# Attention inside a four-block kernel: the row maximum is subtracted by TensorE in PSUM instead of by VectorE

## The reference

```python
qkv = win @ w_qkv + b_qkv                       # win: (256 windows, 49, 32)
attn = jnp.einsum('whnd,whmd->whnm', q, k) * scale
attn = jax.nn.softmax(attn, axis=-1)            # over the 49 keys
out = jnp.einsum('whnm,whmd->whnd', attn, v)
out = out @ w_proj + b_proj
```

## Time and profile before

| | us |
|---|---|
| median of 3 runs (470.24 to 478.76) | 473.28 |
| the profiled execution, its own time | 475.85 |
| its span in the profile | 474.1 |
| mean granted TensorE clock | 0.901 |
| busy: PE, DVE, ACT, POOL | 351.1, 365.1, 299.8, 233.9 |

### The profile page before, as it was taken

The page is one execution under the profiler, slowest core; times in us unless marked ns, Lnnn a source line. Parts: engine busy times, 40 slices in busy tenths (PEclk is TensorE's granted clock), DMA queues, the critical chain, the costliest instruction groups (busy, mean ns, idle before and its releaser), DMA issues. The chain is left out here.

```text
span 474.1 us, 10021 instructions
## 1 busy us (share of the span) xinstructions
PE 351.1 (74%) x3480; PEld 230.4 (49%) x3480; DVE 365.1 (77%) x679; ACT 299.8 (63%) x583; POOL 233.9 (49%) x217
## 2 busy tenths in 40 slices
PE   5149888896789785985877647666795829888885
PEld 4037676675665332142233213222483519877774
DVE  3799999999797388799787999997576685544443
ACT  4327788887785899578758946347985253333432
POOL 4526868775673324966972999567081130000000
PEclk9997999998899999599897885768999668999999
DMA  6110000000223231022000000000030000111111
GB/s 147 5 18 3 3 1 0 0 1 0 59 60 70 51 87 29 1 60 58 1 0 1 0 1 0 0 0 1 3 68 3 1 0 11 20 19 22 22 19 24
DMA packets 24044, 10.29 MB, mean 22 GB/s; under 512 B 20576, under 2 KB 22368, under 8 KB 24016
## 3 DMA queue, kind: packets, MB, share of 16 engines
q1 hardware_dynamic: 23888, 9.93, 10.3%
q0 software_dynamic: 128, 0.01, 0.2%
HBM read 2.00 MB, written 1.61 MB: 8 GB/s over the span
## 5 line engine op out<-in xcount | busy, mean ns | idle before, releaser
L480 POOL TENSOR_TENSOR Pr<-Pr,rc 128x392 f32<-128x392 f32 x64 | 54.4, 883 | 32.2 <-DVE rc L1826 32.2
L511 POOL TENSOR_TENSOR YA<-YA,hC 128x784 f32<-128x784 f32 x27 | 51.7, 1914 | 32.4 <-DVE hC L1910 31.5
L1349 PE MATMUL pair<-BCf,sel 96*128 96x392 bf16 x128 | 38.4, 394 | 35.0 <-DVE Hs L1894 30.8
L1894 DVE TENSOR_TENSOR_SCAN Hs<-dA,pair 128x784 f32<-128x784 f32 x32 | 57.1, 1785 | 1.0
L1193 PE MATMUL pair<-ident,Pr 128*128 128x128 f32 x256 | 41.1, 293 | 13.2 <-ACT PT L715 9.0
L1349 PEld LDWEIGHTS pair<-BCf,sel 96*128 96x128 bf16 x128 | 10.2, 105 | 74.0 <-issue 71.6
L1193 PEld LDWEIGHTS pair<-ident,Pr 128*128 128x128 f32 x256 | 29.2, 146 | 25.1 <-ACT PT L715 15.8
L1887 DVE TENSOR_TENSOR pair<-DU,pair 128x784 f32<-128x784 f32 x32 | 31.1, 973 | 10.6 <-PE pair L1349 10.3
L715 ACT ACTIVATE PT<-pair 128x392 f32<-128x392 f32 x64 | 31.4, 497 | 5.9 <-PE pair L1193 5.6
L724 ACT ACTIVATE Pr<-Ts 128x392 f32<-128x392 f32 x64 | 32.5, 536 | 3.4 <-DVE Ts L1810 3.4
L1804 DVE TENSOR_REDUCE mx<-pair 128x8 f32<-128x392 f32 x64 | 32.6, 550 | 1.6 <-PE pair L1150 1.4
(11 more groups left out here) (262 smaller groups left out, 928.8 us busy)
## 6 DMA issues: line engine op xcount, KB each, us to landing
SX<-XP SPq DMA_DIRECT2D x48, 112.2 KB
XT<-in_x SPq DMA_DIRECT2D x4, 392.0 KB, 5.0
out<-Os SPq DMA_DIRECT2D x28, 56.0 KB, 1.8
AD<-Aa SPq DMA_DIRECT2D x4, 196.0 KB
NB<-in_L_conv_x_proj_w SPq DMA_DIRECT2D x4, 3.0 KB
DW<-in_L_conv_dw SPq DMA_DIRECT2D x4, 1.1 KB
vec<-in_L_conv_b_qkv POOLq DMA_DIRECT2D x3, 0.5 KB, 5.8
W<-in_L_conv_w_qkv SPq DMA_DIRECT2D x1, 48.0 KB
```

The costliest lines, as they stand in the source:

```text
L480: eng.tensor_tensor(pg, pg, bcast(rc[:, g, :], 2, WT), ALU.mult).then_inc(pn_r, 1)
L511: eng.tensor_tensor(y, y, hC[:, n % NHC, :], ALU.add).then_inc(g_ya, 1)
L1349: ins = eng.matmul(SPREAD[s][:, columns(h)], sel[:, n, :], upper(BCf[:, c % 2, s, columns(h)]), start=True, stop=True)
L1894: eng.tensor_tensor_scan(Hs[:, n % 2, :], dA[:, n % NA, :], SPREAD[0], 0.0, ALU.mult, ALU.add).then_inc(v_s, 1)
```

## The change

The subtraction on DVE, its output tile `Ts` and its semaphore `sub_r` go. In their place, for each part of two groups: PE turns the maxima (`mx`, now 32 columns a part, 16 used) with an identity in float32, twice, into two 32-row blocks of bank 7 (`turn_max`); DVE copies the 64 rows to the bfloat16 tile `MT`, and then overwrites rows 32 to 63 by what the rounding left (`pieces`); PE multiplies `MT` by a fixed bfloat16 matrix `msel` of 0 and -1 and adds the product onto the scores in banks 2 * part and 2 * part + 1 (`shift`). ACT takes the exponent from PSUM. The banks of the scores are given back by the exponent. ACT's order becomes t0, t1, t2, e0, t3, e1, e2, e3; PE's new steps stand between the transposes; DVE's order becomes maxima 0, 1, 2, pieces 0, maximum 3, pieces 1. `av` also waits for the last piece. POOL builds `msel` and clears `MT` and `mx` once, ahead of the first strip. The two later waits on `sub_r` in the convolution block are now on `exp_r`.

```diff
-        Ts = sb("Ts", [P, G, 8, WT], att)
+        MT = sb("MT", [64, 2, P], att, BF16)
+        mrow = sb("mrow", [64, 16], att)
+        msel = sb("msel", [64, 2, 8, WT], att, BF16)
...
-        mx = sb("mx", [P, G, 8], att)
+        mx = sb("mx", [P, 2, 32], att)
...
+        QP = 64 + WT
+
+        def shift_rows(part):
+            return banks[7][0:64, 256 + P * part:256 + P * part + QP]
...
+            eng.memset(MT[:], 0.0)
+            eng.memset(mx[:], 0.0).then_inc(s_mk2, 1)
+            eng.wait_ge(s_mk, 5)
+            eng.tensor_tensor(mrow[:, :], ident[0:64, 0:16], ident[0:64, 32:48], ALU.add).then_inc(s_mk2, 1)
+            eng.wait_ge(s_mk2, 6)
+            eng.tensor_scalar(msel[:, :, :, :].rearrange("p g m k -> p (g m) k"), bcast(mrow[:, :], 2, WT), -1.0, None, ALU.mult).then_inc(s_mk2, 1)
...
                 def exponent(g):
-                    eng.wait_ge(sub_r, 4 * s + g + 1)
+                    eng.wait_ge(sh_r, 4 * s + g + 1)
                     if not fixed or s >= 2:
                         eng.wait_ge(t_r, 4 * (s - 2) + g + 1)
-                    eng.activation(Pr[:, par, g, :, 0:WT], Ts[:, g, :, :], ACT.Exp).then_inc(exp_r, 1)
+                    eng.activation(Pr[:, par, g, :, 0:WT], banks[g][:, 0:392].rearrange("p (m k) -> p m k", k=WT), ACT.Exp).then_inc(exp_r, 1)
 
                 turned_out(0)
+                turned_out(1)
+                turned_out(2)
                 exponent(0)
-                turned_out(1)
+                turned_out(3)
                 exponent(1)
-                turned_out(2)
-                turned_out(3)
                 exponent(2)
                 exponent(3)
...
                     if not fixed or s >= 1:
-                        eng.wait_ge(sub_r, 4 * s - 2 + 2 * part)
+                        eng.wait_ge(exp_r, 4 * s - 2 + 2 * part)
...
-                                                 start=True, stop=True)
+                                                 start=pair == 0, stop=False, skip_group_check=True)
                     ins.then_inc(s_r, 1)
+
+                def turn_max(part):
+                    eng.wait_ge(max_r, 8 * s + (2, 6)[part])
+                    if part == 0 and (not fixed or s >= 2):
+                        eng.wait_ge(ao_r, s - 1)
+                    for piece in range(2):
+                        ins = eng.matmul(shift_rows(part)[32 * piece:32 * piece + 32], mx[:, part, :], ident[:, 0:QP], start=True, stop=True,
+                                         skip_group_check=True)
+                    ins.then_inc(mt_r, 1)
+
+                def shift(part):
+                    eng.wait_ge(max_r, 8 * s + (5, 8)[part])
+                    for g in (2 * part, 2 * part + 1):
+                        eng.matmul(banks[g][:, 0:392], MT[:, part, :], msel[:, g % 2].rearrange("p m k -> p (m k)"),
+                                   start=False, stop=True, skip_group_check=True).then_inc(sh_r, 1)
...
                     eng.wait_ge(ring_r, base + G)
+                    if cur:
+                        eng.wait_ge(max_r, 8 * s + 8)
...
                 if prv:
                     transposes(0)
+                turn_max(0)
+                if prv:
                     transposes(1)
                 if early:
                     early()
+                shift(0)
+                turn_max(1)
                 if prv:
                     transposes(2)
+                shift(1)
+                if prv:
                     transposes(3)
                 if prv2:
                     project()
...
-                    for part in range(2):
-                        groups = (2 * part, 2 * part + 1)
-                        eng.wait_ge(s_r, 2 * s + part + 1)
-                        for g in groups:
-                            eng.tensor_reduce(mx[:, g, :], banks[g][:, 0:392].rearrange("p (m k) -> p m k", k=WT), AX.X,
-                                              ALU.max).then_inc(max_r, 1)
-                        for g in groups:
-                            eng.wait_ge(max_r, 4 * s + g + 1)
-                            if not fixed or s >= 1:
-                                eng.wait_ge(exp_r, 4 * (s - 1) + g + 1)
-                            eng.tensor_tensor(Ts[:, g, :, :], banks[g][:, 0:392].rearrange("p (m k) -> p m k", k=WT),
-                                              bcast(mx[:, g, :], 2, WT), ALU.subtract).then_inc(sub_r, 1)
+                    def largest(g):
+                        if g % 2 == 0:
+                            eng.wait_ge(s_r, 2 * s + g // 2 + 1)
+                        if not fixed or s >= 1:
+                            eng.wait_ge(mt_r, 2 * s - 1 + g // 2)
+                        eng.tensor_reduce(mx[:, g // 2, 8 * (g % 2):8 * (g % 2) + 8], banks[g][:, 0:392].rearrange("p (m k) -> p m k", k=WT), AX.X,
+                                          ALU.max).then_inc(max_r, 1)
+
+                    def pieces(part):
+                        eng.wait_ge(mt_r, 2 * s + part + 1)
+                        eng.tensor_copy(MT[:, part, 0:QP], shift_rows(part)).then_inc(max_r, 1)
+                        eng.wait_ge(max_r, 8 * s + (4, 7)[part])
+                        eng.tensor_tensor(MT[32:64, part, 0:QP], shift_rows(part)[32:64], MT[32:64, part, 0:QP], ALU.subtract).then_inc(max_r, 1)
+
+                    largest(0)
+                    largest(1)
+                    largest(2)
+                    pieces(0)
+                    largest(3)
+                    pieces(1)
```

More of the change, by code:

```diff
@@ L210, in build @@
         qk_d, v_r, s_r, t_r, av_r, pj_r, q_r, k_r, exp_r, ring_r = sems("qk_d v_r s_r t_r av_r pj_r q_r k_r exp_r ring_r")
-        xw_r, km_r, pn_r, max_r, sub_r, sum_r, rec_r, ao_r, x1_r = sems("xw_r km_r pn_r max_r sub_r sum_r rec_r ao_r x1_r")
+        xw_r, km_r, pn_r, max_r, mt_r, sh_r, sum_r, rec_r, ao_r, x1_r = sems("xw_r km_r pn_r max_r mt_r sh_r sum_r rec_r ao_r x1_r")
         PRODUCTS = "conv x2 u z delta xB xC out var wout".split()
@@ L1152, in scores @@
                                                  Km[C * g:C * g + C, par, 2 * pair + half].rearrange("p h k -> p (h k)"),
-                                                 start=True, stop=True)
+                                                 start=pair == 0, stop=False, skip_group_check=True)
                     ins.then_inc(s_r, 1)
+                def turn_max(part):
+                    if not cur:
+                        return
+                    eng.wait_ge(max_r, 8 * s + (2, 6)[part])
[6 more added lines that the diff above has]
+                def shift(part):
+                    if not cur:
+                        return
+                    eng.wait_ge(max_r, 8 * s + (5, 8)[part])
+                    for g in (2 * part, 2 * part + 1):
+                        eng.matmul(banks[g][:, 0:392], MT[:, part, :], msel[:, g % 2].rearrange("p m k -> p (m k)"),
+                                   start=False, stop=True, skip_group_check=True).then_inc(sh_r, 1)
                 scores(0)
@@ L1241, in _ @@
             pe_att(-1, 1)
+            eng.wait_ge(s_mk2, 7)
             for s in (0, 1, 2):
@@ L1283, in conv @@
                 if b == 0 and h == 0:
-                    eng.wait_ge(sub_r, 4 * NS - 2)
+                    eng.wait_ge(exp_r, 4 * NS - 2)
                 for y in taps:
@@ L1308, in delta @@
                 if b == 0:
-                    eng.wait_ge(sub_r, 4 * NS)
+                    eng.wait_ge(exp_r, 4 * NS)
                 eng.matmul(result("delta", b)[:, h, :], BD[:, U_DL, :], US[:, b, HT * h:HT * h + HT], start=True, stop=True).then_inc(p_["delta"], 1)
```

## The result

| | us |
|---|---|
| before, median of 4 runs beside it (470.24 to 478.76) | 475.08 |
| after, median of 4 runs (497.78 to 502.99) | 500.25 |
| ratio, 95% interval | 1.0537 [1.0482, 1.0592] |
| span of the profiled execution, before and after | 474.1, 496.0 |

The change makes the kernel about 25 us slower; the profiled execution took 497.78 us. Two of the ten executions of before_psum_exponent, further down, took 772.44 and 773.6 us; no trace of them was kept, nothing on record explains them, and its ratio is taken over the others. The first thing to read is the page of after: the clock row, and the groups that answer to the earlier trace rows and to the addition.

What follows compares the result with a forecast made beforehand. Two loops of nearly one length, DVE's list and POOL, PE, DVE, were taken to hold the strip. 14 steps of +1.6 us, +0.3 and about +1.2 make +24: 473.28 + 24 = 497 us, range 485 to 511.

Steps and rivals of the forecast that it cites:

- Two loops: The strip before, 6.69 us, is held by two loops of nearly one length: DVE's own list, and POOL, PE, DVE.
- the loop through POOL: POOL's four multiplications, last transposes, project, addition to X, sums, inverse, POOL again: 6.60 us, holding none of the subtractions.
- Turn (steps 2 and 5): PE's float32 products turning the maxima: 0.45 us per part, bounds 0.30 and 0.62, plus 0.14 back to DVE.
- Pieces 0 (step 3): DVE's copy and difference for the first part: 0.50 us until DVE can start the next operation.
- The cover: DVE idle about 0.7 us before the second copy, 1.7 before the addition, POOL over 3; ACT's order and bank release hidden.
- Strip 12: In the step to it, new work fits the hole of ACT's table loads, except the second shift: +0.3 us.
- Strip 0: The first strip has the same path to its sums without transposes, at the low clock: about +1.2 us.
- Strips 1, 11 and 13: The steps to these strips were priced like the other ordinary steps, +1.6 us each.
- the clock rival: PE waits more often and the clock falls to 1.2 GHz: over half of the strips +16 us, 513 us; chance 0.12.
- The sum: 14 steps of 1.6 are 22.4 us; with +0.3 and about +1.2, together +24 us, 497 us on the median.
- POOL's loop as the bound of the changed kernel: Rival: POOL's loop goes on setting the strip at 6.60 us, time within a microsecond or two of 473; chance 0.08.
- DVE's list alone: Rival: DVE's list is the bound and PE answers beside it; strip falls 0.9 us, time to 460 us; chance 0.03.

Runs made afterwards that it cites:

- before_psum_exponent: Kernel before, with only subtraction in place in PSUM, exponent from PSUM, banks given back by the exponent and ACT's new order: 474.26 us, ratio 0.9988.
- before_no_subtract: Kernel before, with DVE's four subtractions a strip left out and the exponent taken of bare scores in PSUM: 470.77 us, ratio 0.9942.
- before_project_early: Kernel before, with project alone moved ahead of transposes 2 and 3 on PE, nothing left out: 474.01 us, ratio 0.9963.
- before_no_subtract_project_early: Kernel before, without subtractions, bare exponent from PSUM, and project moved ahead of transposes 2 and 3 on PE: 466.39 us, ratio 0.9811.
- after_project_early: Changed kernel, with project ahead of the first shift on PE and the addition to X ahead of the second pieces on DVE: 498.88 us, ratio 1.0476.
- before_wait_only: Kernel before, with PE holding the last transposes until DVE's fourth subtraction, no new work: 495.38 us, ratio 1.0403.

## Why the prediction was right, and where its steps were off

The time, the sign and the mechanism came out as forecast: 8.28 us were forecast for a strip and 8.21 measured. Of the +24 us that were summed, 22.7 were for the steps from strip to strip, which grew by 23.0, and 1.2 for strip 0; to strip 15 the kernel was 21.8 us late. The steps of the path, from the maximum at 71.31 to the one at 79.39:

| step | predicted | measured |
|---|---|---|
| 1, maxima, to PE | 1.07 | 1.10 |
| 2, turn_max 0 and back | 0.59 | 0.43 |
| 3, pieces 0 | 0.50 | 0.61 |
| 4, maximum 3, to PE | 0.60 | 0.62 |
| 5, turn_max 1 and back | 0.59 | 0.44 |
| 6, pieces 1, to PE | 0.63 | 0.63 |
| 7, shift 1 | 0.44 | 0.44 |
| 8, transposes 3 and project to the addition | 1.13 | 1.16 |
| 9, addition | 0.34 | 0.34 |
| 10, sums and inverses | 2.39 | 2.31 here, 2.61 in the next strip |

- **Two loops, not one.** Right. before_no_subtract shows it from one side (0.03 us less a strip), before_project_early from the other (0.17 less), before_no_subtract_project_early with both (0.23 less). They were not quite equal: the loop through POOL was the longer.
- **Turn (steps 2 and 5): mis-sized.** 0.39 us long and answered after 0.43 to 0.44, predicted 0.45 and 0.14 more. The two products, onto different 32 output rows, ran beside each other. The 0.14 of the way back was taken from project's row; here the copy starts 0.04 to 0.05 us after the modelled end. The Trainium skill, "TensorEngine Tiling (Array Packing)", section "Key Properties", says that tiles operate independently; the 0.39 for four passes agrees.
- **Pieces 0 (step 3): mis-sized the other way.** The prediction let the next operation start at start-to-start pace after 0.50; the maximum started 0.61 after the copy (72.84 to 73.45), behind the whole of both. The errors of steps 2, 3 and 5 come to -0.31 and +0.11; with 0.03 each on steps 1 and 8, 0.02 on step 4 and 0.07 on step 10 (mean 2.46 of the two strips) the steps add to 8.23; the mean strip is 8.21.
- **The cover.** Idle time of DVE ahead of the second copy 0.49 (forecast about 0.7), ahead of the addition 1.65 (1.7), of POOL ahead of its multiplications 3.04 and 3.35 (over 3). DVE busy 10.26 us in 14.50 is 11.6 in two strips of 16.4 (11.5 in 16.6). ACT's order and the bank release cost nothing, as before_psum_exponent shows.
- **Strip 12: wrong sign.** +0.3 was added; it gave 1.40 back. The prediction kept the hole of the table loads where it was. In after, ACT comes to them sooner after POOL's start (131.11 to 132.03, 0.92 us, against 1.96 before), the chain of turns and pieces runs while they load, and the granted clock over the step was 1.00 against 0.82. The sooner loads alone do not do it. In after_project_early they start 1.01 us after POOL, but project stands ahead of the first shift and holds it up until 136.38, behind the loads; the clock was 0.84 and the step took 10.94 us, 0.33 more than before. before_psum_exponent, which has ACT's new order and no turns, starts them 0.07 us after POOL and gives 1.65 back at a clock of 0.69. How the 1.40 divides between the loads, the order behind them and the clock stays open.
- **Strip 0: over-priced; in this trace it even came early.** +1.2 was added for a path at the low clock. That path, from DVE's first maximum to POOL's start, grew only from 5.51 to 5.81 us, but in this execution the maximum itself came 1.55 us earlier. The traces show where: nine small operations on DVE (L1759 before, L1800 after) ran beside POOL's first masking before, and ahead of it after. The rows are of the timeline, first of before, then of after.

```profile
23.99 1.50 POOL L474 TENSOR_TENSOR Km<-Ks,mask 128x784 f32<-128x784 f32 x1 [2.16 <-ACT Ks L706]
24.04 2.81 DVE L1759 TENSOR_SCALAR NB<-W8X,DW 128x32 f32<-128x32 f32 x9
```

```profile
23.77 1.41 DVE L1800 TENSOR_SCALAR NB<-W8X,DW 128x32 f32<-128x32 f32 x9
...
25.18 1.50 POOL L487 TENSOR_TENSOR Km<-Ks,mask 128x784 f32<-128x784 f32 x1 [1.67 <-ACT Ks L719]
```

  The early start is not the change's doing alone. after_project_early does the same work as after up to this point. There DVE waited for a DMA (`DW`) until 23.46 us, the nine operations ran beside the masking again (2.82 us), the first maximum came at 32.33 and POOL started at 38.02, 0.67 us later than in before; its path was 5.69. Over the four traces with the new setup the first maximum came at 30.29, 31.54, 31.72 and 32.33, over the eight of kernels made from before at 31.60 to 31.84. So the path grew by 0.2 to 0.3 us in place of 1.2, and the 1.55 us lie within the scatter of this start, 2.0 us over four traces of the same work. The new setup itself is nearly hidden: PE's first products came 1.19 us later in after (21.37 before, 22.56 after), but 0.68 of that was there when DVE began to normalise the input (18.83 and 19.51), about when POOL's new work began (19.48), and the other 0.52 is this step beside that work, 3.00 us in place of 2.48.
- **Strips 1, 11 and 13: under-priced.** They took +3.22, +2.71 and +2.86 in place of 1.6, 4.0 us more in sum. In the steps to 11 and 13 the statistics and the padding copies stand in DVE's list ahead of the maxima. PE waits for them, and then runs part of the step at the lower of its two levels. The granted clock over these steps was 0.83 and 1.00 before, 0.85 and 0.85 after. So to strip 13 the lower clock is new. To strip 11 it was there before, and what is new is that PE's steps behind the wait now lie on the path. In the step to strip 1 there is no such work. There the clock was even lower before (0.64) than after (0.81); PE makes the scores late, behind the V step that now stands after strip 0's second shift, and the first maximum starts 1.69 us after POOL (36.10 to 37.79) in place of 0.54. The timeline of after, ahead of strip 11:

```profile
123.49 0.39 PE L1176 MATMUL pair<-ident,mx 128*32 128x113 f32 x4 [2.11 <-DVE mx L1846]
...
125.56 1.12 PE L1225 MATMUL pair<-ident,Pr 128*128 128x128 f32 x4
...
126.61 0.83 PE L1185 MATMUL pair<-msel,MT 64*128 64x392 bf16 x2
```

  Transposes that take 0.66 us in the steady strips take 1.12, a shift 0.83 for 0.50. This is the clock rival in small: it came in steps with an extra wait, not in half of them. The steady window kept a clock of 1.00, and the mean over the whole execution was 0.901 before and 0.902 after.
- **The sum.** 14 steps of 1.6 were forecast. Ten took 1.49 each, strip 4 only 0.72, strips 1, 11 and 13 came to 8.8 in place of 4.8, strip 12 to 1.7 less than forecast. Together the steps come to 23.0 where 22.7 were forecast, because these errors cancel, which is luck. The 1.2 for strip 0 was too much, and its trace happened to start early by about as much. The steady strip is right because of its terms, within the errors of steps 2, 3 and 5.
- **The rivals.** POOL's loop as the bound of the changed kernel fell with the gap of 5.15 us between POOL's start and the last transposes. DVE's list alone, with the strip 0.9 us shorter, fell with the longer strip itself, and before_no_subtract shows that even without PE's answers DVE's relief shortens the strip by 0.03 us only.

## What to carry to other kernels

Before work is taken off the busiest engine, walk the other loops of the steady state from an instruction to its next instance: if one is as long, the relief buys idle time. What a hand-over to another in-order engine costs is not the length of the new instruction but the round trip at its place in that engine's queue, plus all that stands behind it; here two lines that only wait cost 4%, and moving the same instructions to other places gave back two thirds of the loss. A wait on PE has a second price, since it can bring the lower clock to the strip behind it (a granted clock of 0.64 behind the 1.61 us in before_wait_only).

## What the hardware showed

- A float32 turn of 113 columns onto two blocks of 32 output rows, four passes in all, takes 0.39 us, where the V step's four passes of 128 columns take 0.69.
- DVE sees PE's answer 0.43 to 0.44 us after the turn starts; PE starts 0.06 us after the second piece ends (75.08 to 75.14). One round trip with the two pieces costs 1.07 us (74.07 to 75.14).
- Where the form of the matmul changes behind the second shift, the transposes start 0.06 us before its end (75.58, end 75.64), as in the earlier trace rows.
- The exponent took 510 ns from PSUM and 536 from SBUF at the same 128x392.
- Nine operations of 128x32 on DVE took 2.81 us beside POOL's masking and 1.41 us without it (rows above), while the masking took 1.50 us in both. All twelve traces of this case agree: 2.72 to 2.86 us in the seven where the masking ran beside them, 1.39 to 1.55 in the five where it was over (but for 0.05 us in one) or had not begun. In each of the seven, one of the nine operations took 1.49 to 1.56 us, as long as the masking itself, and the others 0.23 to 0.39: the traces read as if DVE stood still for one operation of POOL.
